# A retention step on TensorE: both chunks' output products in one place, states released by their own semaphore

## The reference

```python
for i in range(4):
    x = layer_norm(X)
    Q, K, V = x @ Wq[i], x @ Wk[i], x @ Wv[i]        # 8 heads of 16
    Q, K = rotate(Q, cos, sin), rotate(K, cos, -sin)
    att = einsum('bnhd,bmhd->bhnm', Q, K) * Dm       # Dm: causal, gamma_h ** (n - m)
    Y = einsum('bhnm,bmhd->bnhd', att, V)
    Y = group_norm(Y) * gn_s + gn_b
    Yr = swish(x @ Wg[i]) * Y @ Wo[i] + X
    X = gelu(layer_norm(Yr) @ W1[i]) @ W2[i] + Yr
```

## Time and profile before

| | us |
|---|---|
| median of 3 runs | 599.06 |
| lowest, highest | 598.79, 599.08 |
| the profiled execution | 599.84 |
| its span | 598.0 |
| outside the span | 1.8 |
| TensorE busy | 539.7 (90%) |
| VectorE busy | 492.8 (82%) |
| ScalarE busy | 359.2 (60%) |
| GpSimd busy | 210.1 (35%) |

### The profile page before, as it was taken

The page is one execution under the profiler, slowest core; times in us unless marked ns, Lnnn a source line. Parts: engine busy times, 40 slices in busy tenths (PEclk is TensorE's granted clock), DMA queues, the critical chain, the costliest instruction groups (busy, mean ns, idle before and its releaser), DMA issues. The chain is left out here.

```text
span 598.0 us, 14018 instructions
## 1 busy us (share of the span) xinstructions
PE 539.7 (90%) x4372; PEld 413.8 (69%) x4372; DVE 492.8 (82%) x1825; ACT 359.2 (60%) x830; POOL 210.1 (35%) x223
## 2 busy tenths in 40 slices
PE   0899999999999999999988897898299999897994
PEld 0666787878878788787866465896155777466992
DVE  6799888988888888888899797788958999993663
ACT  2677887777877778777767675686234220132760
POOL 2354353442533425335250055375200000072671
PEclk9999999999999999999999999899699999998999
DMA  8949999993000000000000311222100000012315
GB/s 304 372 141 189 180 184 179 186 188 58 3 1 2 2 2 3 2 1 2 2 2 2 103 43 55 80 78 76 32 0 1 2 0 2 1 50 58 101 54 158
DMA packets 61130, 43.29 MB, mean 72 GB/s; under 512 B 4641, under 2 KB 58273, under 8 KB 60801
## 3 DMA queue, kind: packets, MB, share of 16 engines
q1 hardware_dynamic: 56160, 35.42, 28.7%
q0 software_dynamic: 2496, 5.13, 2.6%
q10 hardware_dynamic: 2400, 1.84, 1.0%
HBM read 18.38 MB, written 24.01 MB: 71 GB/s over the span
## 5 line engine op out<-in xcount | busy, mean ns | idle before, releaser
L471 POOL TENSOR_TENSOR att<-att,small 128x512 f32<-128x512 f32 x63 | 80.7, 1282 | 170.7 <-ACT att L360 170.7
L368 ACT ACTIVATE xz<-resid,nmr,rs 128x128 f32<-128x128 f32 x128 | 56.7, 503 | 8.6 <-DVE nmr L838 8.6
L1042 POOL DMA_INDIRECT rows_back<-ffn_yt,ffn_front x46 | 47.0, 1021 | 41.5 <-DVE ffn_yt L1393 40.3
L360 ACT ACTIVATE att<-banks 128x512 f32<-128x512 f32 x63 | 38.3, 607 | 38.3 <-PE banks L518 38.3
L1222 PE MATMUL banks<-ffn_xtT,ffn_wt 128*128 128x128 f32 x368 | 51.7, 286 | 2.2 <-DVE ffn_hr L1387 2.2
L709 DVE TENSOR_TENSOR att<-banks,small 128x512 f32<-128x512 f32 x64 | 44.0, 688 | 9.3 <-PE banks L518 9.1
L1222 PEld LDWEIGHTS banks<-ffn_xtT,ffn_wt 128*128 128x128 f32 x368 | 47.4, 202 | 3.1 <-ACT ffn_wt L1069 2.4
L518 PE MATMUL banks<-qexp,qkT 32*128 32x256 f32 x512 | 45.7, 426 | 1.7 <-DVE att L709 1.2
L489 POOL TENSOR_TENSOR qk<-cosq,sinq 128x512 f32<-128x512 f32 x32 | 40.9, 1277 | 13.9 <-DVE cosq L765 13.5
L894 PE MATMUL banks<-small 128*128 128x512 f32 (+1 forms) x74 | 31.4, 543 | 13.6 <-POOL osc_taps L1465 11.5
L1033 POOL DMA_INDIRECT rows_in<-ffn_front,ffn_slot x32 | 31.9, 998 | 29.0 <-DVE ffn_slot L1305 20.5
(11 more groups left out here) (259 smaller groups left out, 1443.8 us busy)
## 6 DMA issues: line engine op xcount, KB each, us to landing
rows_in<-zero_rows SPq DMA_DIRECT2D x16, 1032.0 KB, 18.3
shared_tab<-in_rot SPq DMA_DIRECT2D x3, 1024.0 KB, 12.6
routed_sb<-in_routed SPq DMA_DIRECT2D x1, 3072.0 KB, 12.3
ffn_front<-rows_in SPq DMA_DIRECT2D x46, 64.5 KB, 1.9
ffn_yg<-rows_back SPq DMA_DIRECT2D x8, 256.0 KB, 3.7
shared_tab<-in_rot ACTq DMA_DIRECT2D x1, 1024.0 KB, 10.3
w<-in_W SPq DMA_DIRECT2D x2, 512.0 KB, 7.3
times<-in_times SPq DMA_DIRECT2D x1, 1024.0 KB, 4.9
```

Source lines behind the costliest of these rows:

```text
L360: act.activation(att[:, c, HALF:HEADS].rearrange("p (r e) n -> p r e n", e=PER_TILE), b_att[:, 2:4, c], ACT.Copy).then_inc(s["att_raw"], 1)
L368: ins = act.activation(xz[:, n], resid[:, (g % GROUPS) * 2 + n % 2], ACT.Identity, scale=rs[:, n:n + 1], bias=nmr[:, n:n + 1])
L471: pool.tensor_tensor(att[:, c, HALF:HEADS], att[:, c, HALF:HEADS], spread(causal.unsqueeze(1), 1, HALF), ALU.mult) \
L1042: pool.indirect_dma_start(rows_back, bass.IndirectOffsetOnAxis(ap=token, axis=0), yt[:, j % RING], None).then_inc(stored[j % RING], 16)
```

## The change

`outputs` no longer takes one chunk. It does both, and it is called once a step, at the place where the second chunk's call stood; the call ahead of the `qk` transposes is gone. Inside it, the two products with the states come first, then the first chunk's eight products, then the second chunk's eight. The waits on the masked scores move from ahead of the product with the state to ahead of the eight.

Each product with a state now counts up a semaphore of its own, `state_read`, and `new_state` waits on that one where it waited on `y_ready`. `y_ready` still counts up once a chunk. Only the first of the two state products has `start` set. To have a semaphore free, `v_mean` is folded into `v_centred`, with counts doubled; this concerns eight small instructions on VectorE.

```diff
-                def outputs(g, v, c):
-
-                    wait(pe, s["state_ready"], 2 * g + c)
-                    if c == 0:
-                        wait(pe, s["yc_sb"], g)
-                    wait(pe, s["att_masked_rest"], 2 * g + c + 1)
-                    wait(pe, s["att_masked"], 2 * g + c + 1)
-                    out = b_y[:, c * P:c * P + P]
-                    pe.matmul(out, state[:, c], qkT[:, v, 0, c], start=True, stop=False,
-                              skip_group_check=True)
-                    for e in range(2):
-                        for q in range(4):
-                            ins = pe.matmul(out[32 * q:32 * q + 32, :],
-                                            ve[:, v, c, q, e].rearrange("p j d -> p (j d)"),
-                                            att[:, c, 2 * q + e, :], start=False, stop=(e == 1),
-                                            skip_group_check=True)
-                    ins.then_inc(s["y_ready"], 1)
+                def outputs(g, v):
+                    wait(pe, s["yc_sb"], g)
+                    wait(pe, s["state_ready"], 2 * g + 1)
+                    for c in range(2):
+                        pe.matmul(b_y[:, c * P:c * P + P], state[:, c], qkT[:, v, 0, c], start=(c == 0), stop=False,
+                                  skip_group_check=True).then_inc(s["state_read"], 1)
+                    for c in range(2):
+                        wait(pe, s["att_masked_rest"], 2 * g + c + 1)
+                        wait(pe, s["att_masked"], 2 * g + c + 1)
+                        for e in range(2):
+                            for q in range(4):
+                                ins = pe.matmul(b_y[32 * q:32 * q + 32, c * P:c * P + P],
+                                                ve[:, v, c, q, e].rearrange("p j d -> p (j d)"),
+                                                att[:, c, 2 * q + e, :], start=False, stop=(e == 1),
+                                                skip_group_check=True)
+                        ins.then_inc(s["y_ready"], 1)
...
-                    if on(2):
-                        outputs(t - 2, (u - 2) % RING, 0)
                     if on(1):
                         g, v = t - 1, (u - 1) % RING
                         if on(7):
...
                     if on(2):
-                        outputs(t - 2, (u - 2) % RING, 1)
+                        outputs(t - 2, (u - 2) % RING)
...
                 def new_state(g, c):
                     wait(dve, s["kv_taken"], 2 * g + c + 1)
                     wait(dve, s["state_ready"], 2 * g + c)
-                    wait(dve, s["y_ready"], 2 * g + c)
+                    wait(dve, s["state_read"], 2 * g + c)
```

More of the change, by code:

```diff
@@ L269, in retention @@
             "gyt_ready", "wo_ready", "xzt_ready", "w1_ready", "w2_ready",
-            "v_mean", "v_centred",
+            "state_read", "v_centred",
             "qkT_sb", "qexp_act", "att_raw", "yT_sb", "yc_sb", "sq_ready", "ynT_sb", "xzT_sb", "v_sb",
@@ L650, in step @@
                             wait(pe, s["hT_sb"], t - 5)
-                        wait(pe, s["v_centred"], 1 + t // GROUPS)
+                        wait(pe, s["v_centred"], 2 + 2 * (t // GROUPS))
                         for c in range(2):
@@ L692, in centre_values @@
                     mean = vmean[:, lo:hi]
-                    dve.tensor_reduce(mean, wv, AX.X, ALU.add).then_inc(s["v_mean"], 1)
-                    dve.wait_ge(s["v_mean"], part + 1)
+                    dve.tensor_reduce(mean, wv, AX.X, ALU.add).then_inc(s["v_centred"], 1)
+                    dve.wait_ge(s["v_centred"], 2 * part + 1)
                     for l in range(lo, hi):
```

## The result

The changed kernel takes 609.35 us in the median of four runs (606.26 to 613.41), the kernel before 599.07. The ratio is 1.0171, with a 95% interval of 1.012 to 1.0222: 7 to 13 us slower. The forecast was 607.6 with a range of 603.5 to 611.0. In two later comparisons, on two chips, where both kernels ran again beside the experiments, the ratio was 1.0122 (1.0093 to 1.015) and 1.0128 (1.0087 to 1.017). The ratios are those of the record, and needn't equal the quotient of the two medians: they differ from it by up to 0.002.

What follows compares the result with a forecast made beforehand. TensorE's own instruction list, waits included, was taken to bound full steps. Full steps 5.7 us plus filling 2.8 plus draining 0 gave 8.5 us over 599.06, so 607.6 us, range 603.5 to 611.0.

Steps and rivals of the forecast that it cites:

- The saving: TensorE's outputs in a full step: both chunks together take 1.54 us against 1.78, saving 0.24 us a step.
- What the move uncovers: Ahead of the qk transposes in full steps: TensorE idles 0.47 us waiting for x_next, formerly covered by the first chunk's outputs.
- The full step: Steps 7 to 31: 0.47 us new idle time less 0.24 saved, net +0.23 us each, 5.7 us over 25 steps.
- No second wait: Behind L597 in a full step: nothing waits again; new_state's product is early by a margin of about 0.1 us.
- The filling: Steps 2 to 6, while the pipeline fills: 0.55 us longer each, 2.8 us in all, bounds 1.4 to 3.3.
- The draining: From step 32 on, where VectorE leads: 0 us, between -0.3 and +0.3.
- The blocks behind: Blocks behind the retention: unchanged, they only move along.
- the switch alone counts: Rival: L597 released at 152.33, each full step 0.24 us shorter, total 593.1 us; chance 4%.
- a draw: Rival: L749 ready some 0.2 us earlier, half the wait goes, total within 1.2 us of 599.06; chance 4%.
- the merging not doing what it says: Rival: second chunk's weights load late, the 0.24 us saving is lost, total 613.6 us; chance 3%.
- A dearer merged place: Rival: extra waits in the merged outputs, 0.1 to 0.2 us more a step, total 610.1 to 612.6 us; chance 12%.
- The filling absorbs: Rival: filling steps lose only 0.2 us each, full steps as forecast, total 605.8 us; part of the forecast's 77%.

Runs made afterwards that it cites:

- with the states early: Changed kernel with only the two state products back ahead of the qk transposes; against the kernel before, 597.58 us, ratio 0.994, and on another chip 596.09 us, ratio 0.9927.

## Why the prediction held, point by point

- **The bound.** TensorE's list sets the full step: every order tried moved the step by what it did to that list and its waits, and in the changed kernel VectorE's wait before L755 took up the rest.
- **The saving.** 1.54 us was forecast for both chunks, 1.55 measured. The worth of a border was sized too small if anything: 0.33 when both calls stand together.
- **What the move uncovers.** 0.47 us idle was forecast, ended by L746 in every full step: 0.47 measured, and L594 waits for L746 in each of the 25. Taking off that wait moved the transposes up to L587.
- **The full step.** +0.23 us forecast, 9.55; measured 9.554, in the three traces of the changed kernel. Over 25 steps 5.7 forecast, 5.8 measured.
- **No second wait.** L605, L616 and the merged outputs don't wait in a full step. `new_state` was held by the state products once in the 25, for 0.4 us: the margin that was worked out as 0.1 held in the others.
- **The filling.** Forecast 0.55 us in each of five steps, 2.8 in all, between 1.4 and 3.3. Steps 3 to 6 measured 0.53 each, 2.12 us together. Step 2 can't be told from the spread at the program's start; beside the kernel with the states early, in the traces of both where the clock is full early, it is 0.44 longer. Step 3 is 0.45 longer than there too, and takes as long there as in the kernel before (7.60). By this my estimate for the five steps is 2.6 us. So the term was sized well. What the sum didn't have is in the profiled execution's 4.7: 1.5 us of half clock at 45 us, and some 0.6 ahead of step 2's projections. The sign "clock at 1.00 throughout the retention" did not come there: it is 0.95 up to 67.22. Its waits are those named. In the list from 20 to 68 us, `new_state` does wait for the state products, and the transposes for GpSimd:

```profile
PE banks L594 <- POOL qk L489: 5.5, 5, 1.6
...
DVE state L732 <- PE banks L526: 2.0, 4, 1.0
```

- **The draining.** 0 forecast, 0.2 measured.
- **The blocks behind.** "Move along" was wrong as a statement on their length: they came out 1.7 us shorter in the profiled execution, and 3.7 and 4.8 us longer with the states early, where the granted clock was lower. The forecast lay 1.75 us under the median of four runs, and the other two comparisons, with +7.0 and +6.8 us where +8.5 was forecast, lie on its other side by as much. Full steps, filling and draining by the traces are 5.8 + 2.6 + 0.2 = 8.6 us, and all three intervals take that in. That the single medians come within 2 us of the forecast is in part luck, since one execution can hold 1.5 us of half clock in the filling and several us behind the retention.
- **The rivals.** That the switch alone counts, a draw, and the merging not doing what it says are excluded by the trace. A dearer merged place is excluded as well: its parts cost what the sum had. "The filling absorbs" (0.2 us a step) falls too, with 0.53 a step.

## What to carry to other kernels

Merging work to save a fixed cost takes it away from one of its places: ask first what each place covered, and from which instant. Here 0.24 us saved uncovered 0.47. Then look for the smallest piece that covers the wait and has the form of its neighbours: two of the 18 products were enough, and the order that keeps those and merges the rest beats both kernels: it is 0.6% and 0.7% faster than the one before in two comparisons, and each interval ends below 1.

To size such a change, compare the same rows in the same steps of several traces. Whole times spread by some us from execution to execution here, the full steps and steps 3 to 6 of the filling by 0.02 us where the clock is full, but for two single steps that took 0.6 and 0.3 us more.

## What the runs showed that was not expected

- On one of the three chips both kernels were 5% slower (631.11 us before). The retention was not: the changed kernel's 25 steps took 238.85 us there, as elsewhere. Its blocks behind it took 291.9 us against 259.7. A ratio from that chip understates a change in the retention, and the trace by stages does not.
- The stretches at half clock fall at different places in different executions of one kernel, and they weigh on the time far from the change: 20 us at 1.2 GHz right behind the retention in one trace with the states early, whose blocks there took 4.8 us more than in the kernel before.
- Two calls of `outputs` in a row cost 0.99 us for the second one, 0.10 more than where another kind of product stands between them.
